# Attention with a gated projection: third groups' first units move to row-tiled maxima and ones-matmul sums, and TensorE's runs are regrouped

## Time and profile before

| | |
|---|---|
| median of 3 runs | 1672.48 us (1672.14 to 1673.76) |
| the profiled execution, its own time | 1672.39 us |
| its span, first to last instruction | 1670.6 us, so 1.8 us lie around it |
| PE busy | 1602.0 us, 96% |
| DVE, ACT, POOL busy | 71%, 72%, 74% |
| granted TensorE clock | mean 0.995; 1.00 in every stretch asked after 400 us |

### The profile page before, as it was taken

How to read it: one execution, slowest core, us unless ns; L and a number is a source line. 1 busy time by engine, 2 the same in 40 slices (tenths; PEclk the granted TensorE clock), 3 DMA queues, 4 the chain that set the end, 5 groups by cost and what they waited for, 6 DMA issues and landing times.

```text
span 1670.6 us, 34222 instructions
## 1 busy us (share of the span) xinstructions
PE 1602.0 (96%) x11931; PEld 685.3 (41%) x11931; DVE 1184.2 (71%) x1790; ACT 1195.6 (72%) x3057; POOL 1239.8 (74%) x1223
## 2 busy tenths in 40 slices
PE   9988999989999899998999999999999989999988
PEld 4333344434444344443444434443344434444433
DVE  7787776787667766686767866678676776667762
ACT  3476787777777777687776787866787777777762
POOL 0277767887788779887688776798768897678865
PEclk9999999999999999999999999999999999999999
DMA  7323312333224422243122532233312322222121
GB/s 214 118 36 74 89 41 64 96 85 76 52 65 98 91 56 52 79 112 79 46 58 71 126 70 49 61 86 101 86 41 63 99 77 63 52 58 71 44 66 51
DMA packets 182951, 125.97 MB, mean 75 GB/s; under 512 B 104734, under 2 KB 157214, under 8 KB 182332
## 3 DMA queue, kind: packets, MB, share of 16 engines
q1 hardware_dynamic: 182300, 123.40, 29.6%
q10 hardware_dynamic: 480, 0.39, 0.1%
HBM read 41.40 MB, written 17.02 MB: 35 GB/s over the span
## 4 chain that ended last, share of the span: by engine, by line
PE 77%; ACT 6%; issue 6%; POOL 4%; DVE 3%; SPq 3%; DMA 1%; POOLq 0%; ACTq 0%; DVEq 0%
PE pJ L576 30%; PE pO L820 13%; PE pJ L801 10%; PE pS L774 3%; PE pJ L797 3%; PE pJ L671 3%; PE pJ L675 3%; PE pJ L672 3%; POOL acc L1311 2%; SPq L1415 2%; PE pS L756 2%; PE pJ L740 2%; ACT pS L940 2%; ACT PT L920 2%; PE pS L757 1%
## 5 line engine op out<-in xcount | busy, mean ns | idle before, releaser
L1311 POOL TENSOR_TENSOR acc<-acc,PT 128x512 f32<-128x512 f32 (+1 forms) x714 | 874.7, 1262 | 15.8 <-PE pO L820 10.8
L920 ACT ACTIVATE PT<-pJ 128x512 f32<-128x512 f32 (+1 forms) x1080 | 614.7, 583 | 328.8 <-PE pJ L801 313.2
L801 PE MATMUL pJ<-QK 97*128 97x512 f16 (+3 forms) x1280 | 384.5, 318 | 5.5 <-ACT acc L920 3.4
L1172 DVE TENSOR_REDUCE mx<-pS 128x3 f32<-128x1536 f32 (+3 forms) x264 | 377.4, 1440 | 0.0
L1156 DVE TENSOR_REDUCE mx<-pS 128x1 f32<-128x384 f32 (+3 forms) x330 | 209.0, 636 | 139.9 <-PE pS L757 138.0
L1168 DVE TENSOR_REDUCE mx<-pJ 128x1 f32<-128x512 f32 (+3 forms) x264 | 151.7, 585 | 180.0 <-PE pJ L774 117.5
L820 PE MATMUL pO<-PT,V 128*32 128x512 f32 (+2 forms) x2800 | 259.4, 484 | 1.1 <-ACT PT L920 1.1
L940 ACT ACTIVATE pS<-pS,a 128x128 f32<-128x128 f32 (+1 forms) x480 | 251.3, 527 | 1.2
L797 PE MATMUL pJ<-QK 128*128 128x128 f16 x1024 | 180.6, 221 | 13.3 <-ACT PT L920 10.0
L576 PE MATMUL pJ<-xT,wh_k 128*128 128x512 f16 x512 | 192.5, 378 | 0.0
L576 PE MATMUL pJ<-wh_v,xT 128*128 128x512 f16 x512 | 189.9, 379 | 1.4 <-ACT acc L920 1.3
(11 more groups left out here) (177 smaller groups left out, 2681.8 us busy)
## 6 DMA issues: line engine op xcount, KB each, us to landing
QK<-sg SPq DMA_DIRECT2D x762, 64.0 KB, 2.0
xs<-in_x SPq DMA_DIRECT2D x60, 256.0 KB, 3.2
xr<-in_x SPq DMA_DIRECT2D x58, 256.0 KB, 3.1
...
QK<-aT SPq DMA_DIRECT2D x256, 1.0 KB, 1.7
...
QK<-in_mqk SPq DMA_DIRECT2D x2, 512.0 KB, 10.0
```

Source lines behind the costliest of these rows:

```text
L801: ins = e.matmul(slot[:, to:to + 512 - q0], k4[0:97, j, kc], q4[0:97, j, q0:512], start=True, stop=True)
L920: e.activation(probabilities_at(i), bank("t", i)[:, 0:cols], ACT.Exp, scale=SS).then_inc(s_p, 1)
L1172: e.tensor_reduce(mx[:, par, part, :].rearrange("p (j q) -> p j q", q=4)[:, 0:3, qi], pS[:, :, c0:c0 + w], AX.X, ALU.max).then_inc(s_m0, 1)
L1311: e.tensor_tensor(a, a, PT[:, RING_AT[i] % NPT, 0:width * len(heads)].rearrange("p (j q) -> p j q", j=len(heads)), ALU.add).then_inc(s_ap, 1)
```

## The change

- The eight first units of third groups leave `ROW` and join `ADDED`. Their 11 chunks with all that follows (L756, L757, L1156, L933, L940, L1419, L1440, L1444) go; three row-tiled batches come at slots 2.0, 5.0 and 8.5 of the period before (`TM["l"]`), and the sums are made directly by ones for kb 0 to 3, just ahead of the unit's `outputs`.
- All first units: `outputs` has one run of four key blocks at slot 11.11, in place of two.
- `row_sums` of odd units move from slot 7.25 to 11.06, right ahead of that run.
- `beside_run` moves a batch that lies within 0.4 slot of a run to just before the run.
- `s_sm` becomes two semaphores, for even and odd units. Staging q and k (`stage_qk` on ACT) waits for the last batch of a third group's first unit, and two waits guard `mx` and `a16` where neighbouring first units now differ in kind.
- Nearly all numbers of `TM` have new values.

```diff
 TM = {
-    "s": ((23.47, 19.19, 14.67, 25.97, 27.78, 32.28, 35.49), (21.14, 23.62, 27.8, 18.53, 32.83, 30.34, 35.56), (26.84, 18.48, 23.42, 20.26, 35.88, 29.2, 34.45), (20.03, 18.16, 22.49, 26.86, 35.91, 34.17, 29.73)),
-    "pv": (1.15, 2.1, 0.32, 1.43, 1.47, 3.64),
-    "x": (-109.63, -108.5, -98.07, -86.65, -71.06, -69.14, -61.84, -49.79),
-    "sm": (2.88, -1.21, -0.25, 4.18),
-    "ln": ((-46.75, -23.74, -21.76, 35.69), (-79.63, 9.97, 7.64, 26.89), (-14.62, 0.37, -6.61, 7.42)),
-    "c": ((0.77, 0.97), (-0.06, 1.16), (0.81, 0.94), (-1.08, 1.16)),
...
+    "s": ((22.65, 19.68, 18.64, 26.07, 32.66, 28.04, 35.58), (23.53, 19.37, 27.7, 18.23, 29.07, 31.93, 35.8), (25.73, 20.9, 23.16, 18.52, 33.55, 31.59, 35.86), (25.8, 18.97, 17.91, 22.74, 34.42, 36.25, 29.28)),
+    "l": (2.0, 5.0, 8.5),
+    "pv": ((0.81,), (0.26, 1.22, 1.49, 4.73)),
+    "x": (-109.14, -108.48, -96.82, -98.88, -71.51, -63.5, -53.94, -50.05),
+    "sm": (4.18, -0.05, -0.22, 3.07),
+    "ln": ((-45.98, -44.83, -26.67, 35.53), (-75.58, 1.01, 0.7, 26.25), (-16.71, -1.17, -10.1, 7.46)),
+    "c": ((1.26, 1.07), (0.34, 1.32), (1.27, 1.39), (-0.84, 1.32)),
...
-ADDED = [n for n in range(NU) if n % NQS or n in EARLY]
+LATE = tuple(n for n in range(0, NU, 2) if n // 2 % NG == 2)
+ADDED = [n for n in range(NU) if n % NQS or n in EARLY or n in LATE]
...
+SNAP = 0.4
+RUNS = ((0, 1, 2, 3),), ((0, 1), (2, 3), (4, 5), (6, 7))
+def run_of(n, kb):
+
+    return next((k, run) for k, run in enumerate(RUNS[n % NQS]) if kb in run)
+
+
+def at_pv(n, kb):
+
+    k, run = run_of(n, kb)
+    return at_t(T_LAST[n, run[-1]]) + TM["pv"][n % NQS][k] + 0.005 * (kb - run[0])
+
+
+RUN_AT = [at_pv(n, run[0]) for n in range(NU) for run in RUNS[n % NQS]]
+
+
+def beside_run(t):
+
+    near = min(RUN_AT, key=lambda r: abs(r - t))
+    return near - 0.03 if abs(near - t) < SNAP else t
+
+
 for _n in range(NU):
     _k = 0
...
-                BATCHES.append((38 * (_n // 2 - 1) + (TM["e"][_n // 2] if _n % NQS == 0 else TM["s"][_n // 2 % NG] if _n > 1 else TM["s0"])[_k], (_n, _part, _blocks)))
+                BATCHES.append((beside_run(38 * (_n // 2 - 1) + (TM["e"][_n // 2] if _n in EARLY else TM["l"] if _n in LATE else TM["s"][_n // 2 % NG] if _n > 1 else TM["s0"])[_k]), (_n, _part, _blocks)))
...
-RING = [i for i, (n, kb, w, hs) in enumerate(T_TILES) if kb > 0 or n not in ADDED]
+RING = [i for i, (n, kb, w, hs) in enumerate(T_TILES) if kb > 0 or n not in ADDED or n in LATE]
...
-DIRECT = {2: (0, 1, 2, 3), NU - 3: (4, 5, 6, 7), NU - 1: (4, 5, 6, 7)}
+DIRECT = {n: (0, 1, 2, 3) for n in LATE}
+DIRECT.update({2: (0, 1, 2, 3), NU - 3: (4, 5, 6, 7), NU - 1: (4, 5, 6, 7)})
...
-def at_pv(n, kb):
-
-    return at_t(T_LAST[n, kb | 1]) + TM["pv"][n % NQS * 2 + kb // 2] + 0.01 * (kb & 1)
+def at_direct(n, kb):
+
+    run = run_of(n, kb)[1]
+    return at_pv(n, run[0]) - 0.02 + 0.005 * (kb - run[0])
...
-    return at_pv(n, DIRECT[n][0] & ~1) - 0.02 if n in DIRECT else at_sums(n)
+    return at_direct(n, DIRECT[n][0]) if n in DIRECT else at_sums(n)
...
-    return at_pv(n, 3) + TM["sm"][0] if n % NQS == 0 else at_pv(n + 1, 1) + TM["sm"][1]
+        return at_direct(n, DIRECT[n][-1])
+    return at_pv(n, 3) + TM["sm"][0] if n % NQS == 0 else at_pv(n + 1, 0) + TM["sm"][1]
...
+        def sums_made(n):
+
+            return s_sm[n % NQS], sum(m % NQS == n % NQS for m in ADDED[:ADD_AT[n] + 1])
...
-                for n in DIRECT:
+                for n in sorted(DIRECT):
                     for kb in DIRECT[n]:
-                        yield at_pv(n, kb & ~1) - 0.02 + 0.01 * (kb & 1)
+                        yield at_direct(n, kb)
                         first, last = T_FIRST[n, kb], T_LAST[n, kb]
...
-                            if o == 0 and 2 * gn - 2 in EARLY:
+                            if o == 0 and 2 * gn - 2 in ADDED:
                                 ln.wait_ge(s_S, last_batch(2 * gn - 2) + 1)
...
-                            ln.wait_ge(s_sm, ADD_AT[n - 2] + 1)
+                            ln.wait_ge(*sums_made(n - 2))
...
+                        if m - 2 in C_LAST:
+                            ln.wait_ge(s_e, C_LAST[m - 2] + 1)
...
-                    if m > 1:
+                    if m - 2 in C_LAST:
+                        ln.wait_ge(s_ac, C_LAST[m - 2] + 1)
+                    elif m > 1:
                         ln.wait_ge(s_a16, ADD_AT[m - 2] + 1)
...
```

More of the change, by code:

```diff
@@ L39 @@
 TM = {
-    "s": ((23.47, 19.19, 14.67, 25.97, 27.78, 32.28, 35.49), (21.14, 23.62, 27.8, 18.53, 32.83, 30.34, 35.56), (26.84, 18.48, 23.42, 20.26, 35.88, 29.2, 34.45), (20.03, 18.16, 22.49, 26.86, 35.91, 34.17, 29.73)),
-    "s0": (18.87, 15.83, 24.28, 21.26, 29.57, 34.63, 37.34),
-    "e": ((-11.39, -7.49, -2.54), (8.61, 12.43, 10.75)),
-    "held": (1.29, 0.24, 1.3, 2.08, 1.93, 1.24, 1.94, 0.62),
[12 rows of a table removed]
-    "gate": (-1.41, -0.66, 6.27, 3.81, 5.71),
-    "ln": ((-46.75, -23.74, -21.76, 35.69), (-79.63, 9.97, 7.64, 26.89), (-14.62, 0.37, -6.61, 7.42)),
-    "mx": (0.66, 0.17, -0.12),
-    "sh": (2.93, 1.96),
-    "c": ((0.77, 0.97), (-0.06, 1.16), (0.81, 0.94), (-1.08, 1.16)),
-    "ex": (0.45, 1.14),
-    "mv": (2.06,),
-    "stage": (-0.82, 0.28),
-    "hl": (-6.39, -0.01),
-    "pr": (-0.09,),
-    "add": (2.82,),
-    "nrm": (-0.6, 0.81, 0.13, -1.25),
-    "out": (1.79, 3.93, 2.42),
-    "hi": ((4.17, 6.06), (2.63, 8.27)),
-    "vst": (0.43,),
-    "res": (0.42, 1.37),
+    "s": ((22.65, 19.68, 18.64, 26.07, 32.66, 28.04, 35.58), (23.53, 19.37, 27.7, 18.23, 29.07, 31.93, 35.8), (25.73, 20.9, 23.16, 18.52, 33.55, 31.59, 35.86), (25.8, 18.97, 17.91, 22.74, 34.42, 36.25, 29.28)),
+    "s0": (18.79, 15.56, 24.7, 21.54, 30.25, 33.84, 37.28),
+    "e": ((-10.01, -7.29, 0.18), (10.03, 11.75, 12.22)),
+    "l": (2.0, 5.0, 8.5),
+    "held": (1.15, -0.29, 1.19, 1.55, 1.41, 0.88, 1.56, -0.14),
[12 rows of a table added]
+    "gate": (-0.39, -1.47, 6.37, 4.32, 6.02),
+    "ln": ((-45.98, -44.83, -26.67, 35.53), (-75.58, 1.01, 0.7, 26.25), (-16.71, -1.17, -10.1, 7.46)),
+    "mx": (0.62, 0.34, -0.12),
+    "sh": (1.58, 1.85),
+    "c": ((1.26, 1.07), (0.34, 1.32), (1.27, 1.39), (-0.84, 1.32)),
+    "ex": (0.15, 1.13),
+    "mv": (2.65,),
+    "stage": (-0.74, 0.18),
+    "hl": (-6.41, 0.17),
+    "pr": (-0.1,),
+    "add": (2.95,),
+    "nrm": (-0.45, 0.52, 2.45, 3.76),
+    "out": (4.06, 4.83, 2.3),
+    "hi": ((7.31, 7.08), (5.0, 8.41)),
+    "vst": (0.16,),
+    "res": (0.37, 1.42),
 }
 EARLY = (0, 2)
-ADDED = [n for n in range(NU) if n % NQS or n in EARLY]
+LATE = tuple(n for n in range(0, NU, 2) if n // 2 % NG == 2)
+ADDED = [n for n in range(NU) if n % NQS or n in EARLY or n in LATE]
 ROW = [n for n in range(NU) if n not in ADDED]
@@ L81, with at_t @@
 T_TILES, T_FIRST, T_LAST = [], {}, {}
+for _n in range(NU):
+    for _kb in range(4 * (_n % NQS) + 4):
+        _w = 512 - max(0, P * (_kb - 4 * (_n % NQS)))
+        _heads = max(h for h in (1, 2, 4) if h * _w <= 512)
+        T_FIRST[_n, _kb] = len(T_TILES)
+        T_TILES += [(_n, _kb, _w, range(j, j + _heads)) for j in range(0, 4, _heads)]
+        T_LAST[_n, _kb] = len(T_TILES) - 1
+def at_t(i):
+    return i + 0.3
+SNAP = 0.4
[9 more added lines that the diff above has]
+    return near - 0.03 if abs(near - t) < SNAP else t
 for _n in range(NU):
@@ L419, in build @@
         s_bp, s_br = sm("s_bp"), sm("s_br")
-        s_xt, s_qk, s_vp, s_fp, s_op, s_sm = sm("s_xt"), sm("s_qk"), sm("s_vp"), sm("s_fp"), sm("s_op"), sm("s_sm")
+        s_xt, s_qk, s_vp, s_fp, s_op = sm("s_xt"), sm("s_qk"), sm("s_vp"), sm("s_fp"), sm("s_op")
+        s_sm = [sm(f"s_sm{i}") for i in range(2)]
         s_hi, s_lo, s_xd = sm("s_hi"), sm("s_lo"), [sm(f"s_xd{i}") for i in range(2)]
@@ L521, in probabilities_at @@
             n, kb, width, heads = T_TILES[i]
-            if kb == 0 and n in ADDED:
+            if i not in RING_AT:
                 return sums_of(n)[:, heads[0], :]
@@ L1212, in outputs @@
                 for n in range(0, NU, 2):
-                    yield at_pv(n, 3) + TM["out"][0] if n not in EARLY else past("sm", n) + TM["nrm"][1] + 1.4
+                    yield at_pv(n, 3) + TM["out"][0] if n in ROW else past("sm", n) + TM["nrm"][1] + 1.4
                     ln.wait_ge(s_pv, units(n + 1))
```

21 lines of the change are left out of this document (6 added, 15 removed), and 18 rows, old and new, of the table TM.

## The result

The changed kernel takes **1686.94 us** (median of 4 runs, 1682.18 to 1691.47), beside 1673.12 us for the kernel before: ratio 1.0083, 95% interval 1.0070 to 1.0097. It is 0.8% slower; the forecast was 1650 with a range up to 1671. The profiled execution took 1682.18 us, span 1680.4.

A forecast was written before the change was run, and what follows sets the result against it. PE's own stream was taken as the bound, with ACT for one stretch in four groups. From 1672.4 us, stream -2.8, waits -18.4, zero row -5 and new waits +4 sum to -22.2: 1650 us, range 1637 to 1671.

The forecast's parts named there:

- term 10: Everything else: changed work on ACT, DVE and SP costs nothing beside PE; new waits of the re-timed order +4 us.
- Terms 1 to 3: On PE, third groups' first units: chunks out -17.9, batches in +11.0, sums by ones +17.8 us.
- Terms 4 and 5: On PE: merged runs save 63 visits at 0.23 us, -14.5 us; batches placed next to runs, +0.8 us.
- Terms 6 to 8: PE's waits in the ACT-bound stretch shrink by 2.6 us in each of seven repeats, -18.4 us.
- term 6: The chunk's 1.1 us wait for the last maxima of the odd unit's batches goes.
- term 7: row_sums come 3.8 slots later, so POOL's additions are done and PE's 0.3 us wait goes.
- term 8: ACT's stretch: of PE's 2.5 us of waits about 1.3 remain; half, 1.25 us, taken as gain.
- Term 9: PE's 7.9 us wait for the row of zeros, in 7 places, shrinks by 3 to 7.9; -5 us taken.
- wrong if the four windows together are not some 2.5 to 3 us shorter: Sign against the forecast: four consecutive group windows not some 2.5 to 3 us shorter than 201.2 us.
- if L774 waits longer in total than 6.7: Sign against the forecast: batches (L774) make PE wait longer in total than 6.7 us.
- The hand-over rival: At the odd unit's first run, slot 18.56, hand-over of pO becomes the wait; 1.5 us on average gives 1697; chance 0.10.
- DVE's reading of batches: PE waits 0.56 us for DVE at each of 24 added batches, +13 us: 1664; chance 0.08.

The follow-up runs named there:

- experiment 13: Changed kernel with the low halves of all 56 x tiles made by a one-tile DVE reduction instead of a two-tile subtraction (x counts double): 1646.81 us.
- 15: Changed kernel with third groups' first units back in chunks (LATE empty) and the reduction for all x tiles: 1637.11 us.
- 3: Changed kernel with batches moved beside runs only before slot 190, afterwards keeping their own times: 1703.85 us.
- 4: Changed kernel with first units' outputs in two runs again and odd units' sums back at slot 7.25: 1844.57 us.
- 8: Kernel before with first units' outputs merged into one run, row_sums ahead of it, and the normalising and output copy times that follow: 1745.21 us.
- without contention: All x-tile subtractions replaced by DVE reductions, which POOL does not shut out: changed kernel 1646.81 us, kernel before with the same edit 1671.24 us.
- the let-in: Changed kernel with POOL waiting once per third group, before one addition, for DVE's subtraction: 1669.43 us.
- experiment 2: Changed kernel with third groups' first units back in chunks (LATE empty), all else as changed: 1674.0 us.
- Experiment 9: Kernel before with only the fifth x tile of each batch entry two slots earlier (-73.06 for -71.06): 1691.44 us.

## Why the prediction was wrong

**The failed step is term 10**: "All lie beside PE and cost nothing while PE is 96% busy", and the +4 for waits of a re-timed order. I counted DVE's work by its mean durations and never asked what makes a duration. The subtraction L1126 was in the trace before: 56 of them, mean 1105 ns where the shortest took 648. Of a stretched duration like this it must be asked who stretches it, and what happens if the neighbour's gap moves. Before, the hole in POOL's chain came 0.9 us after the subtraction's start (773.7 after 772.8). In the changed kernel the subtraction starts 6.4 us into the third group's period in place of 9.4 (772.21 - 765.8, and 772.78 - 763.4), while the hole moved from 10.3 to 12.0, so it comes 5.6 us after the start. A wait of 4 to 5 us on DVE then passes over ACT to PE, and half clock follows. I bounded new waits by the idle of good windows (0.5 us a period). Measured, as the difference of the changed kernel's periods to those of experiment 13: 3.8 to 5.4 us in each of the five long third groups, some 2 us in each second one, and 40 us in all by experiment 13 (1686.94 - 1646.81).

- **Terms 1 to 3** (-17.9, +11.0, +17.8) are right. By the windows of 13 and 15 the moved units cost 2.1 us of sums in the third group (2.22 forecast) and save 0.8 in the second (2.23 - 1.38 = 0.85): +1.3 a group, +10 in all (1646.81 - 1637.11 = 9.7).
- **Terms 4 and 5**: the sums do stand ahead of the run without a full matmul between, and the visit has the forecast's price. In the changed kernel's timeline of PE:

```profile
930.70 0.38 PE L711 MATMUL pJ<-wh_o,Onl 128*128 128x512 f16 x1
931.01 1.06 PE L776 MATMUL pJ<-acc,ones 128*32 128x512 f32 x8
...
934.17 0.39 PE L837 MATMUL pJ<-QK 97*128 97x512 f16 x1
```

  From 930.70 to 934.17 are 3.47 us; less 0.22 for L711, 0.86 for the sums and 2.15 for the 1280 columns of the run, 0.24 us are left for one visit, where a period of the kernel before has three. The first and fourth groups' periods, which have no wait now and hardly had one, shrank by 0.6 and 1.0 us; two visits at 0.23 make 0.46 of either. The rest, with the batches beside runs (term 5), was not isolated: 3, 4 and 8 added waits that drown it.
- **Terms 6 to 8** (-2.6 us per repeat): without contention the second and third group together have 1.5 + 2.15 us of idle, 1.4 below the 2.0 + 3.0 of before: half of the forecast, -10 in place of -18.4. By the waits of these two periods, in the kernel before and in experiment 13: term 6 is right (1.1 us gone), **term 7** is wrong (`row_sums` come 3.8 slots later, but POOL's chain is not done: 0.3 became 0.9 us; 1.4 in the changed kernel, 1.8 with the let-in), and of term 8's 2.5 us of waits for ACT 0.9 go, where half was taken.
- The moved units do not bring those gains: 15 has the same idle as 13. The rest of the change does.
- **Term 9** (zero row, -5): -7.3 in the changed kernel, near its upper bound of 7.9, and -6.0 in experiment 13.
- **The sum**: without contention four groups take 197.1 us against 200.6, -3.5, where 2.5 to 3 was forecast; -24.4 us in all against -22.2. The counting of streams held, and what it left out was larger than the sum. That the totals are so near is partly luck: terms 6 to 8 brought 8 us less than forecast, the +4 of new waits did not come, and the periods without waits shrank more than by their visits.
- **Signs named ahead**: "wrong if the four windows together are not some 2.5 to 3 us shorter" (204.1 for 200.6) and "if L774 waits longer in total than 6.7" (14.9) both came (the undisturbed four groups: 199.8). The hand-over rival did not: L856 waits for `On` once, 1.1 us. (Its price had a slip: 31 x 0.7 us on top of 1650 is 1672, level with the kernel before and not slower.) DVE's reading of batches as a rival had the right place in second groups and the wrong reason: experiment 13 brings that wait from 14.9 to 8.3 us without touching one batch, and experiment 2, without the added batches, leaves it at 13.7.

Open: why DVE gets in at the next boundary of two POOL instructions in most places and is passed by four or five in others. Five of the seven cases of the changed kernel differ by nanoseconds: by the trace's single records, which are rough for POOL, an addition starts 0 to 5 ns before the subtraction in the three that are held, and 6 ns before in the two that are not. The spread of the kernel's runs (1682 to 1691) may come from this; it is not shown. Experiment 9 forced it in two of seven only.
